# Softmax and weighted values of the first two edge blocks among the later blocks' gathers

## What is computed

```
xp = (x @ W_gat).reshape(n, H, C)
alpha = jax.nn.leaky_relu(a_src[src] + a_dst[dst], NEG_SLOPE)
m = jax.ops.segment_max(alpha, dst, num_segments=n)
ea = jnp.exp(alpha - m[dst])
denom = jax.ops.segment_sum(ea, dst, num_segments=n)
attn = ea / (denom[dst] + 1e-16)
msg = xp[src] * attn[..., None]
out = jax.ops.segment_sum(msg, dst, num_segments=n)
return out.mean(axis=1) + bias_gat
...
h = layer_norm(h + x, g1, be1)
ff = jax.nn.relu(h @ w1 + b1) @ w2 + b2
return layer_norm(ff + h, g2, be2)
```

## Time and profile before

| | |
|---|---|
| median of 3 runs | 3396.81 us (3395.88 to 3410.65) |
| profiled execution, its own time | 3399.81 us |
| span of its instructions | 3398.0 us |
| POOL busy | 2533.3 us (75%), 2011 instructions |
| PE busy | 2270.3 us (67%) |
| DVE busy | 1842.4 us (54%) |
| ACT busy | 862.2 us (25%) |
| mean granted TensorE clock | 0.773 |

### The profile page before, as it was taken

How to read it: one execution, slowest core, us unless ns; L and a number is a source line. 1 busy time by engine, 2 the same in 40 slices (tenths; PEclk the granted TensorE clock), 3 DMA queues, 4 the chain that set the end, 5 groups by cost and what they waited for, 6 DMA issues and landing times.

```text
span 3398.0 us, 34863 instructions
## 1 busy us (share of the span) xinstructions
PE 2270.3 (67%) x10329; PEld 1608.8 (47%) x10329; DVE 1842.4 (54%) x3167; ACT 862.2 (25%) x1636; POOL 2533.3 (75%) x2011
## 2 busy tenths in 40 slices
PE   2886777747777777777777475566561587887750
PEld 1554455535555555565555354445440244454430
DVE  4788878883433434333333232322248998797730
ACT  1332222212333232322323122222221122222220
POOL 7788888887887878787777787887840038888877
PEclk9888888877888787777877676676665798787775
DMA  2322222221111112121111111111100001111100
GB/s 57 85 70 70 68 71 65 48 63 31 33 38 35 38 37 41 36 41 35 38 27 32 26 24 24 24 27 20 23 16 0 30 15 29 32 26 28 33 10 10
DMA packets 116073, 123.70 MB, mean 36 GB/s; under 512 B 70597, under 2 KB 72618, under 8 KB 115941
## 3 DMA queue, kind: packets, MB, share of 16 engines
q0 software_dynamic: 64000, 30.57, 9.4%
q1 hardware_dynamic: 51940, 91.52, 8.4%
HBM read 59.51 MB, written 64.00 MB: 36 GB/s over the span
## 4 chain that ended last, share of the span: by engine, by line
POOL 65%; issue 19%; DVE 8%; PE 7%; DMA 0%; DVEq 0%; ACT 0%; POOLq 0%; ACTq 0%
POOL ring L409 44%; POOL x_table L431 14%; POOL out_rows L457 6%; DVE region L1457 2%; PE V L773 1%; PE C L525 1%; PE V L513 1%; DVE region L1449 1%; DVE region L1123 1%; DVE region L1433 1%; DVE region L1385 0%; PE C L773 0%; DVE region L1408 0%; DVE region L1405 0%; PE C L519 0%
## 5 line engine op out<-in xcount | busy, mean ns | idle before, releaser
L409 POOL DMA_INDIRECT ring<-in_x,index x800 | 1042.6, 1303 | 244.3 <-issue 244.0
L457 POOL DMA_INDIRECT out_rows<-ring,index_out x400 | 510.0, 1275 | 370.3 <-DVE ring L1264 250.6
L1092 DVE TENSOR_REDUCE var<-sq 125x16 f32<-125x512 f32 x325 | 220.4, 681 | 839.9 <-ACT sq L838 734.9
L409 POOL DMA_INDIRECT ring<-x_table,index x400 | 492.0, 1230 | 124.4 <-issue 124.1
L431 POOL DMA_INDIRECT x_table<-region,index_out x400 | 485.7, 1214 | 121.9 <-issue 121.9
L838 ACT ACTIVATE sq<-C 125x512 f32<-125x512 f32 x300 | 179.4, 598 | 961.9 <-PE C L525 416.5
L513 PE MATMUL V<-xT,w_q 128*128 128x500 f32 x600 | 365.3, 762 | 53.5 <-ACT xT L830 25.7
L474 PE MATMUL T<-ident,hrow 125*128 125x125 f32 x1000 | 196.3, 335 | 194.4 <-DVE hrow L1108 171.8
L525 PEld LDWEIGHTS C<-w_c,hid 128*125 128x125 f32 x2400 | 320.1, 219 | 0.0
L525 PE MATMUL C<-w_c,hid 128*125 128x32 f32 x2400 | 319.4, 296 | 0.0
L489 PE MATMUL C<-center,xT 128*125 128x128 f32 x1400 | 258.6, 347 | 78.5 <-DVE hrow L1114 47.2
(11 more groups left out here) (223 smaller groups left out, 3421.6 us busy)
## 6 DMA issues: line engine op xcount, KB each, us to landing
ring<-in_x,index POOLq DMA_INDIRECT x800
nodes<-in_x SPq DMA_DIRECT2D x25, 500.0 KB
x_table<-nodes SPq DMA_DIRECT2D x25, 500.0 KB
x_plain<-nodes SPq DMA_DIRECT2D x25, 500.0 KB
nodes<-x_plain SPq DMA_DIRECT2D x50, 250.0 KB
out_rows<-nodes SPq DMA_DIRECT2D x50, 250.0 KB
x_table<-region,index_out POOLq DMA_INDIRECT x400
ring<-x_table,index POOLq DMA_INDIRECT x400
```

The source lines that it names most:

```text
L409: pool.indirect_dma_start(out=ring[0:P, j, s * F:(s + 1) * F], out_offset=None, in_=table, in_offset=bass.IndirectOffsetOnAxis(ap=index[0: ...
L457: pool.indirect_dma_start(out=out[:, :], out_offset=bass.IndirectOffsetOnAxis(ap=index_out[0:P, j, s:s + 1], axis=0), in_=ring[0:P, j, s * ...
L1092: v.tensor_reduce(unit(var, k), slots(squares(k)), AX.X, ALU.add).then_inc(var_ready, 1)
```

## The change

The first two blocks (EARLY = 2, units 0 to 9) get their softmax and their values inside the gather stage, and the other three blocks get their softmax among the outputs of block 0.

- The gather stage is written out turn by turn on PE, ACT and DVE, in place of a loop over blocks. Behind turns 10, 11 and 12 stand the parts of the softmax over the first two blocks, with tiles of 125 x 1280. Behind each of turns 13 to 22 stands `x_early` for one unit: the values on two banks (V0 and V1; the hidden layer has the other two), without the copy to `stage`. Behind turn 17 block 0's segments are closed.
- The segment that is open where block 1 ends can't be normalised yet. Its unnormalised sums are kept per head: `alpha_open` holds the weights of those slots, PE adds up x rows by them (`open_sums`, 16 small products a unit, 8 rows by 32 columns), and `y_first` scales the sums once the whole maximum and sum are known (`gap`, `ratio`, `total`), and sends them through the heads' weights as the carry into block 2.
- `y_first` replaces the softmax, `e_block(0, None)` and the first round of the loop: outputs of block 0 with the softmax of blocks 2 to 4 (tiles of 125 x 1920) between them, then block 1's closing scan.
- `e_block` follows for (2, 1), (3, 2), (4, 3) and (none, 4), written out.
- SP no longer waits for the softmax before the first loads of x1 and base rows; it still waits for all plain node units to be stored.

New helpers on DVE split the old `join` and the old softmax lines: `join_rows` is its part on 8 partitions, `join_slots` its part on the slots, `below_max`, `denominators` and `weights` are the subtraction, the scans of the sums, and the reciprocal with its product, each for `n` blocks from block `lo` on. `whole_first` reads the first segment's total over the seam.

The diff, cut to its core (first PE's, then DVE's functions of the same names):

```diff
+EARLY = 2
+E1 = EARLY * P * SE
+X_FROM = NJ * EARLY + 3
+FIRST_JOIN, SECOND_JOIN = (2, 3), (5, 6)
+X_END = (4, 7, 8, 9, 10)
...
-            sp.wait_ge(softmax_done, 1)
...
+            def open_sums(c):
+
+                at, bank = cq.next()
+                pe.wait_ge(c_done, cq.room)
+                for i in range(CE):
+                    e = c * CE + i
+                    m = mm(C[bank][0:H, 0:F], alpha_open[0:P, :, e], diff[0:P, e * F:(e + 1) * F],
+                           start=i == 0, stop=i == CE - 1, skip_group_check=True)
+                m.then_inc(c_ready, 1)
...
+            def x_early(c):
+                if c == 0:
+                    pe.wait_ge(softmax_done, 1)
+                t = transpose(diff[0:P, c * W:(c + 1) * W])
+                open_sums(c)
+                for g in range(G):
+                    x_values(t, EARLY_T[c % 2], g, V)
+                if c == NJ - 1:
+                    x_tail_T(X_END[0])
+                    x_carry_T(X_END[0])
...
+            for b in range(NB):
+                for w in range(NJ):
+                    d_turn(b, w, first=b + w == 0)
+                    at = b * NJ + w
+                    if at == X_FROM - 3:
+                        ends_T(EARLY, FIRST_JOIN[0])
+                        carries_T(EARLY, FIRST_JOIN[0])
+                    if at == X_FROM - 2:
+                        ends_T(EARLY, FIRST_JOIN[1])
+                    if at == X_FROM - 1:
+                        carries_T(EARLY, FIRST_JOIN[1])
+                    if X_FROM <= at < X_FROM + EARLY * NJ:
+                        x_early(at - X_FROM)
...
+            def x_early(c):
+                at, rows = bank_ready()
+                if c == 0:
+                    v.tensor_copy(open_sum, rows[0:H, 0:F]).then_inc(c_done, 1)
+                else:
+                    dve.wait_ge(c_done, at + CREDIT)
+                    v.tensor_tensor(open_sum, open_sum, rows[0:H, 0:F], ALU.add).then_inc(c_done, 1)
+                pending = []
+                x_products(c, 0, pending, V)
+                x_products(c, 1, pending, V); x_sum(c, pending)
+                x_products(c, 2, pending, V); x_sum(c, pending)
+                x_products(c, 3, pending, V); x_sum(c, pending); x_sum(c, pending)
+                if c == NJ - 1:
+                    x_tail(0)
+                    x_carry(0)
+                    x_on(0)
+
+            cq.restart(); steps.restart(); vq.restart(); rq.restart()
+            vq.depth = 2
+            for b in range(NB):
+                for w in range(NJ):
+                    d_turn(b, w, first=b + w == 0)
+                    at = b * NJ + w
+                    if at == X_FROM - 3:
+                        for j in range(NJ):
+                            dve.wait_ge(rows_landed[j], NB * DMAS)
+                            dve.wait_ge(x1_saved[j], 16 * NB)
+                        for k in range(2):
+                            dve.wait_ge(base_saved[k], 16 * NB * (3 - k))
+                        to_segments(slots_of(self_logit, 0, EARLY), 0, EARLY)
+                        join_rows(0, EARLY, ALU.max, FIRST_JOIN[0], max_in)
+                    if at == X_FROM - 2:
+                        join_slots(slots_of(self_logit, 0, EARLY), 0, EARLY, ALU.max, FIRST_JOIN[0])
+                        below_max(0, EARLY)
+                        denominators(0, EARLY, 0)
+                    if at == X_FROM - 1:
+                        join_rows(0, EARLY, ALU.add, FIRST_JOIN[1], sum_in)
+                        join_slots(denom_of(EARLY), 0, EARLY, ALU.add, FIRST_JOIN[1])
+                        weights(0, EARLY, 0)
+                        v.tensor_tensor(alpha_open[0:P, :, :], slots_of(beta, 0, EARLY), open_end[0:P, :].unsqueeze(1).to_broadcast([P, H, EARLY * SE]),
+                                        ALU.mult).then_inc(softmax_done, 1)
+                    if X_FROM <= at < X_FROM + EARLY * NJ:
+                        x_early(at - X_FROM)
+            d_turn(NB, 0, last=True)
...
+            def y_first():
+                late = NB - EARLY
+                own, other = slots_of(self_logit, EARLY, late), denom_of(late)
+                y_sum(0, 0)
+                to_segments(own, EARLY, late)
+                y_norm(0, spread(2))
+                y_sum(0, 1)
+                join_rows(EARLY, late, ALU.max, SECOND_JOIN[0], max_in)
+                whole_first(late, ALU.max, total)
+                step(v.tensor_tensor(gap, total, max_in, ALU.max))
+                step(v.tensor_tensor(gap, max_in, gap, ALU.subtract))
+                y_norm(1, spread(2))
+                y_finish(0, 0, spread(3))
+                join_slots(own, EARLY, late, ALU.max, SECOND_JOIN[0])
+                below_max(EARLY, late)
+                dve.sem_inc(ratio_ready, 1)
+                y_sum(0, 2)
+                y_norm(2, spread(2))
+                y_finish(0, 1, spread(3))
+                denominators(EARLY, late, 3)
+                y_sum(0, 3)
+                dve.wait_ge(exp_ready, 8)
+                step(v.scalar_tensor_tensor(out=sum_out, in0=own_in, scalar=1e-16, in1=sum_in, op0=ALU.add, op1=ALU.add))
+                step(v.tensor_tensor(sum_out, sum_out, ratio, ALU.mult))
+                v.tensor_tensor(own_in, own_in, ratio, ALU.mult)
+                step(v.tensor_tensor(sum_in, sum_in, ratio, ALU.mult))
+                join_rows(EARLY, late, ALU.add, SECOND_JOIN[1], sum_in)
+                whole_first(late, ALU.add, total)
+                step(v.scalar_tensor_tensor(out=total, in0=own_in, scalar=1e-16, in1=total, op0=ALU.add, op1=ALU.add))
+                step(v.reciprocal(total, total))
+                step(v.tensor_tensor(total, total, sum_out, ALU.mult))
+                v.tensor_scalar(open_scaled, open_sum, total, None, ALU.mult).then_inc(open_ready, 1)
+                y_norm(3, spread(2))
+                y_finish(0, 2, spread(3))
+                join_slots(other, EARLY, late, ALU.add, SECOND_JOIN[1])
+                y_sum(0, 4)
+                weights(EARLY, late, 3)
+                dve.sem_inc(softmax_done, 1)
+                y_norm(4, spread(2))
+                y_finish(0, 3, spread(3))
+                x_tail(1)
+                y_finish(0, 4, spread(3))
+                x_carry(1)
+                dve.wait_ge(rows_T, 2 * (X_END[1] - 2) + 2)
+                _, rows = bank_ready()
+                v.tensor_copy(tails_row[0:F, 0:1], rows[0:F, 0:1]).then_inc(c_done, 1)
+                step(v.memset(carry_last[0:F, :], 0.0))
+
+            y_first()
...
+            for y in range(1, NB):
+                e_block(y + 1 if y + 1 < NB else None, y)
```

More of the change, by code:

```diff
@@ L965, in _, with ends_rows @@
-            tq.restart(); cq.restart(); tq.depth, cq.depth, fq.depth = 1, 1, 2; fq.restart()
-            def x_stage(c):
-                nc.scalar.activation(stage[0:P, :], diff[0:P, bass.ds(c * W, W)], ACT.Copy).then_inc(stage_ready, 1)
+            def ends_rows(n):
+                ends, _, _ = row_values(n)
+                for k in range(0, 2 * n, 4):
+                    size = min(4, 2 * n - k) * P
+                    evac(ends[:, 1 + k * P:1 + k * P + size], rows=H, width=size)
+                act.wait_ge(t_done, tq.at + 1 + CREDIT)
+                act.sem_inc(rows_T, 1)
@@ L1443, in x_products @@
+            def x_products(c, g, pending, banks):
                 rq.next()
```

558 lines of the change are left out of this document (318 added, 240 removed).

## The result

The changed kernel took 3315.27 us (median of 4 runs, 3313.47 to 3321.84) beside 3401.06 us for the kernel before on the same chip: a ratio of 0.9748, 95% interval 0.972 to 0.9776. The profiled execution took 3314.93 us with a span of 3313.1.

| us | predicted | measured |
|---|---|---|
| end of the gather stage (its last scan) | 2606 | 2598.8 |
| L, its lateness against 2536.0 of before | 70 | 62.8 |
| A, from there to unit 5's first scatter | 203 | 207.9 |
| from there to the end | 505 | 506.4 |

A forecast was written before the change was run, and what follows sets the result against it. It took POOL's issue of indirect DMAs as the bound: gather stage's end 2536 + 70 of lengthening + 203 to unit 5 + 505 of POOL's time = 3314 us of span, forecast 3313 us, range 3260 to 3380.

The forecast's parts named there:

- the two places without scatters: Behind the last gather: 101 us of softmax and 62 us of block 0's weighted values, within POOL's wait of 248.8 us.
- softmax 24: Gather stage, turns 10 to 12: the first two blocks' softmax adds 47 us less 18 slack and 5 overlap: 24.
- Value work 50: Gather stage, turns 13 to 22: ten units at 11 us, less 30 us of slack a block, add 50 us.
- Closing of block 0 10: Gather stage, turn 17: block 0's closing scan, tail and carry add 7.1 us and about 3 of transposes: 10.
- Given back 14: Gather stage: slack of turns 23 and 24 returns 12 us and a better PE clock 2.
- The lower bound, 25: Least lengthening of the gather stage, 25 us, if turns overlap at the lower price of 7.3 us a unit.
- Rival 1: The gather stage absorbs the new work and grows by only 25 us: time 3268, chance 0.17.
- Rival 2: The gather stage grows by 100 to 130 us; at 16.3 us a unit, 123 and time 3366; chance 0.2.
- Rival 3: Gather stage: value work makes the kernel slower, deciding at 154 us, 19.5 a unit; chance 0.06 slower, 0.06 within 0.5%.
- The softmax's part, 54: Between the outputs of units 0 to 4: DVE does three blocks' softmax, 0.6 x 89.4 = 54 us.
- The lower bound of 185: Gather stage's end to unit 5, POOL alone: first fill 38, five units 126, scans that hold it up 20.
- The rule on two inputs: Behind the gather stage: VectorE instructions with two SBUF inputs would hold scatters, lower bound 208 instead of 185; not adopted.

The follow-up runs named there:

- the sums twice: Changed kernel with the four sums over heads of each early value unit done twice on DVE: 3402.85 us, ratio 1.0005.
- interleaved: Changed kernel with the early value units' four parts done between the steps of the next gather turn: 3330.36 us, ratio 0.9787.

## Why the prediction was right

**The bound.** The chain, POOL's waits and the two places without scatters were read rightly. POOL was not stopped in the gather stage: its last gather is at 2517.8, near 2514. From unit 5 on it never waits, and 506.4 us stand against 505. That the sum, 3314, is within 1 us of the measured span of 3313.1 is in part luck: L was 7 us too high, A 5 and the rest 1 too low.

**L, 70 against 62.8.** By its terms: softmax 24, measured 22.7 (turn 13 ends that much later than in before). Value work 50, measured 41: a block without its closing part takes 143.3 us against 122.8. Closing of block 0 10, measured 10.4. Given back 14, measured 11, which is only the balance of the other terms to 62.8. The value term is too high by 9, about 1 us a unit. I had priced the 16 small products at 3.6 us from the rows of L525, and they took 1.5 to 1.7 (15.2 us for 288 records). The remark behind the sum, that L would be nearer 50 if the clock rose with the fuller stage, had the direction right: it rose from 0.71 to 0.87, and the Trainium skill's rule ("TensorE: Matmul & The Clock Gate", What's actually happening) agrees with that, and with both edits of the small products. In the prediction's own unit, slack included, the value work came to (20.6 + 30) / 5 = 10.1 us where I took 11. The lower bound, 25, doesn't follow from its own price: 7.3 us a unit gives 24 + 13 + 10 - 14 = 33. On DVE's timeline the first unit lasts 14.6 us, from 2285.9 to 2300.5; so some 4.5 of it must lie beside PE's and ACT's steps of the next turn, an estimate from the two.

**Rivals 1 to 3.** The stage does absorb work up to the slack of its turns: without the value work the last scan stands as close behind the last gather as before, and 7 us of lengthening are left, in the gathers. Once the slack is used up every further us counts in full (82.3 for 80). Rival 1 overrated the slack, since it took DVE's idle time for usable. Rival 2's 16.3 us a unit was wrong because DVE's waits at the two banks are short: 17.8 us in all over the ten units, 1.3 the longest. Rival 3's point is shown at 18 us a unit.

**A, 203 against 207.9.** The wait for the loads is 5.5 (predicted 5), though only 3.4 of it is worth anything. First fill 35.0 (38). Block 1's first output sum starts 157.4 us behind the last scan where I had 153, and from there to its fill it takes 49.5 where I had 50, so the miss lies among the outputs of block 0. The softmax's part, 54, counts DVE's work on 8 partitions too; its slot work alone is 44.2 us busy and worth 37.4. The lower bound of 185 was made with three scan groups that hold scatters for 0.6 x 7.2 us each; those are contiguous scans, beside which scatters took 1.3 to 1.7 us. This changed nothing, as DVE sets A. What I had not in the sum is the clock behind the stage: the same code takes 208, 210 or 217 us.

**The rule on two inputs.** The prediction kept the trace's bound against the rule of the Trainium skill, "SBUF — State Buffer", Who interferes with whom. That reading was wrong, though the time didn't hang on it. The one row it went by (1.23 us beside the product at 2836.23) was not typical: the same trace has a scatter held beside such a product, DVE's row first:

```profile
2818.66 0.69 DVE L1264 TENSOR_TENSOR ring<-nodes,hrow 125x512 f32<-125x512 f32 x1
```

```profile
2818.79 1.63 POOL L457 DMA_INDIRECT out_rows<-ring,index_out  x1 [0.30 <-issue]
```

It ends 1.07 us behind the product. The eleven scatters beside the wide products bear the rule out: a contiguous product with two inputs in SBUF holds a scatter for the length of that instruction, and the reciprocal with one input holds none. The contiguous scans of 80 slots, which have two inputs and held nothing, are the exception; their 32 took 7.01 us together. In size it is less than the prediction had made of it: what the products cost a scatter is 0.7 to 1.25 us, 9.6 us for the eleven, where 23 were put on the lower bound. The long holds, over a whole group, come with the step of 32 floats alone. In the gather stage of the changed kernel the one gather that was held for over 2 us stood beside block 0's closing scans, DVE's row first:

```profile
2407.41 7.17 DVE L1262 TENSOR_TENSOR_SCAN region<-cont,region 125x80 f32<-125x80 f32 x32
```

```profile
2409.81 5.85 POOL L428 DMA_INDIRECT ring<-x_table,index  x1 [0.30 <-issue]
```

## What to carry to other kernels

Where a queue that issues transfers sets the end, price a move by three dates: when the stage ahead ends, when the first unit that runs in steady order is ready, and how long the queue takes from there. Work put into a stage with room is free up to the slack of its chain of engines and costs one for one beyond it; idle time inside that chain is not slack, and laying the work finer did not make it so. If PE is partly idle and on the path, read the granted clock beside the time of every edit there: here PE work added or taken away was mostly given back by the clock, and the stage behind came out 9 us longer in some kernels and not in others, for a reason that stayed open.

## What was not expected of the hardware

- Fifteen of 16 small products a unit left out made the kernel 17 us slower (3334.53 against 3317.78 us), and doubling them left it where it was (3319.03); 9.2 of the 17 us are later code in which 32 products took 6.76 instead of 3.86 us.
- That later code takes 207.8 to 207.9 us or 217.0 to 217.1, each repeated in two traces of one kernel. The kernels with the sums twice (217.0) and interleaved (217.1) have the longer time too, and the one without the value work lies between (210.3). Why a kernel gets the one or the other is open.
- Where the gather stage begins varied between 1898 and 1915 us in traces of kernels whose code ahead of it is the same. The three latest (1914.8, 1910.1 and 1908.7) had the clock at 0.77, 0.78 and 0.78 from 800 to 1900 us, those that began by 1904.4 had 0.79 or 0.80; the one kernel that I ran again didn't repeat it.
- Groups of DVE work with a step of 32 floats made an indirect transfer's issue take 4.6 to 8.0 us instead of 1.2, until 1.1 us behind the group. A contiguous instruction with two inputs in SBUF made it take up to 2.44 us, until 1.1 us behind that one instruction; contiguous scans of 80 slots and a reciprocal of 12 us did nothing to it.
